# A four-layer graph network on one core: preparation split into four parts, waits dropped from the attention sweep, scan rows stored without gaps, and another release for the relation sweep's marks

## What is computed

```
L0: msg = relu([x[src], x[dst], w] @ W1 + b1) @ W2 + b2 ; agg = segment_max(msg, dst) ; relu([x, agg] @ U1 + c1) @ U2 + c2
L1: msg = relu([x[src], factors[dst]] @ Wm + bm)         ; agg = segment_sum(msg, src) ; x + relu([x, agg] @ Wc + bc)
L2: four heads: e = leaky_relu(e_l[src] + e_r[dst]) ; softmax of e over the edges of a receiver ; sum of alpha * Wh[src]
L3: twice: neigh = mean over edges of h[src] ; h = h @ W[0] + neigh @ W[1] (relu after the first)
```

## Time and profile before

| | us |
|---|---|
| median of 3 runs (lowest, highest) | 6593.26 (6587.62, 6595.1) |
| profiled execution: time | 6596.86 |
| profiled execution: span, first to last instruction | 6595.1 |
| busy: POOL, PE, DVE, ACT | 3886.5 (59%), 3682.2 (56%), 2495.9 (38%), 1392.2 (21%) |
| DMA, mean over the span | 165 GB/s |

### The profile page before, as it was taken

The page is one execution under the profiler, slowest core; times in us unless marked ns, Lnnn a source line. Parts: engine busy times, 40 slices in busy tenths (PEclk is TensorE's granted clock), DMA queues, the critical chain, the costliest instruction groups (busy, mean ns, idle before and its releaser), DMA issues. The chain is left out here.

```text
span 6595.1 us, 101052 instructions
## 1 busy us (share of the span) xinstructions
PE 3682.2 (56%) x19907; PEld 2827.0 (43%) x19907; DVE 2495.9 (38%) x4067; ACT 1392.2 (21%) x3059; POOL 3886.5 (59%) x3936
## 2 busy tenths in 40 slices
PE   1258888896587777636666564233333343333334
PEld 1145565564465555435555554123323332332332
DVE  4223333334344444525655555422222212222224
ACT  0012222222122232212222222111111111111111
POOL 0467777776200000667777774577777757777775
PEclk9679999998799999767878777555555565555556
DMA  9369999993355555256656563344544434444452
GB/s 343 123 193 293 291 296 292 298 297 105 122 182 182 186 182 171 81 124 171 168 156 168 156 169 103 92 126 125 127 126 125 126 86 126 125 127 126 125 127 75
DMA packets 1080339, 1090.67 MB, mean 165 GB/s; under 512 B 128353, under 2 KB 867622, under 8 KB 1076854
## 3 DMA queue, kind: packets, MB, share of 16 engines
q1 hardware_dynamic: 398532, 393.02, 20.3%
q10 hardware_dynamic: 546204, 390.09, 19.1%
q0 software_dynamic: 135456, 306.11, 18.5%
HBM read 662.62 MB, written 427.19 MB: 165 GB/s over the span
## 5 line engine op out<-in xcount | busy, mean ns | idle before, releaser
L1040 POOL DMA_INDIRECT gath<-sender_table,idx x1664 | 1657.6, 996 | 547.4 <-issue 376.0
L1247 DVE TENSOR_TENSOR_SCAN scan<-meta,scan,bank 128x512 f32<-128x512 bf16 x624 | 798.6, 1280 | 2086.1 <-DVEq L1244 2083.0
L1116 PE MATMUL bank<-ident,gath 128*128 128x128 f32 x1664 | 464.1, 434 | 1367.3 <-DMA gath<-sender_table,idx 1367.3
L1463 POOL DMA_INDIRECT gath<-attention_table,idx x832 | 852.3, 1024 | 349.3 <-issue 226.7
L1040 POOL DMA_INDIRECT gath<-joint_table,idx x832 | 850.3, 1022 | 273.6 <-issue 213.0
L1116 PEld LDWEIGHTS bank<-ident,gath 128*128 128x128 f32 x1664 | 297.7, 217 | 1533.4 <-DMA gath<-sender_table,idx 1533.4
L682 POOL COPY idx<-end_i 128x4 int32<-128x4 int32 (+1 forms) x65 | 13.5, 207 | 1040.5 <-POOLq L681 1040.3
L1184 ACT ACTIVATE rows<-bank 128x512 f32<-128x512 f32 x624 | 372.7, 597 | 1101.7 <-ACTq L1183 1059.1
L1142 PE MATMUL bank<-ident,scan 128*128 128x128 f32 x2496 | 570.1, 374 | 5.0 <-PEq L1140 5.0
L1142 PEld LDWEIGHTS bank<-ident,scan 128*128 128x128 f32 x2496 | 471.7, 203 | 132.0 <-issue 132.0
L1123 PE MATMUL bank<-ident,gath 128*128 128x128 f32 x1664 | 374.8, 310 | 0.0
(11 more groups left out here) (245 smaller groups left out, 6065.8 us busy)
## 6 DMA issues: line engine op xcount, KB each, us to landing
recv<-receiver_rows SPq DMA_DIRECT2D x624, 256.0 KB
scan_rows<-rows ACTq DMA_DIRECT2D x624, 256.0 KB
attention_scan_rows<-rows ACTq DMA_DIRECT2D x208, 264.0 KB
receiver_rows<-gath ACTq DMA_DIRECT2D x26, 2048.0 KB, 11.2
meta<-edge_meta SPq DMA_DIRECT2D x208, 256.0 KB
factor_rows<-gath ACTq DMA_DIRECT2D x208, 256.0 KB
gath<-factor_rows SPq DMA_DIRECT2D x208, 256.0 KB
scan_rows<-rows SPq DMA_DIRECT2D x208, 256.0 KB
```

Of the source, the lines that this page charges most:

```text
L1040: pool.indirect_dma_start(out=landed[s][:, c, 0:width], out_offset=None, in_=table[:, :], in_offset=bass.IndirectOffsetOnAxis(ap=idx[s][:, ...
L1116: ins = pe.transpose(b[:, c * P:(c + 1) * P], g[:, c, 0:F], ident[:, :])
L1247: chain(v.tensor_tensor_scan(scan[s % 2][:, :], go_on, src, scan[1 - s % 2][:, EB - 1:EB], ALU.add if k == 1 else ALU.mult, ALU.max if k = ...
L1463: pool.indirect_dma_start(out=gath[s][:, c, :], out_offset=None, in_=att_d[:, :], in_offset=bass.IndirectOffsetOnAxis(ap=idx[s][:, c:c + 1 ...
```

## The change

1. **Preparation in parts.** The 52 node tiles are taken in four parts (12, 14, 14, 12). DVE counts tiles of part g, releases POOL for part g's gathers, and then counts inside part g-1, on one semaphore per part. The edge marks and the rest stay.
2. **Scan rows put together.** Where only features are kept, `rows[s]` is written and stored as 4 x 128 floats without gaps (rows_flat), in edge phases 1, 4, 5 and the relation sweep.
3. **Relation sweep.** The marks are loaded right behind the wait on e_recv_free; e_meta_free is no longer used there. PE issues go_row before the senders.
4. **Attention sweep.** Marks and receiver rows share one wait on SP. The free semaphores of same, er, msg, hid, pre, scan and back are no longer raised or waited for, and scores no longer waits for its own end (one semaphore t_added is waited for once per stretch). PE and ACT take turn_back / keep_rows ahead of turn_weighted / keep_weighted; DVE takes scores ahead of same_receiver.

```
+        rows_flat = [r[:, :, :].rearrange("p c f -> p (c f)")[:, 0:CT * F].rearrange("p (c f) -> p c f", f=F) for r in rows]
...
+            quarter = (0, 12, 26, 40, NT)
...
+                    for g in range(4):
+                        pool.wait_ge(tiles_ready, 1)
+                        pool.sem_inc(tiles_ready, -1)
+                        for t in range(quarter[g], quarter[g + 1]):
+                            pool.indirect_dma_start(out=found[:, t, :], out_offset=None, in_=dst_d[:, :],
+                                                    in_offset=bass.IndirectOffsetOnAxis(ap=tiles_i[:, t:t + 1], axis=0),
+                                                    bounds_check=last_row, oob_is_err=False).then_inc(found_in[g], 16)
...
+                    def count_tiles(lo, hi):
...
+                        chain(v.tensor_scalar(tiles[:, lo:hi], tiles[:, lo:hi], float(T - 1), None, ALU.min))
+                        chain(v.tensor_copy(tiles_i[:, lo:hi], tiles[:, lo:hi]))
+                        v.sem_inc(tiles_ready, 1)
+
+                    def count_inside(lo, hi, g):
+                        v.wait_ge(found_in[g], 16 * (hi - lo))
...
+                    for g in range(5):
+                        if g < 4:
+                            count_tiles(quarter[g], quarter[g + 1])
+                        if g > 0:
+                            count_inside(quarter[g - 1], quarter[g], g - 1)
```

The relation sweep, SP's load and PE's steps:

```
-                        sp.wait_ge(e_meta_free, 1)
-                        sp.sem_inc(e_meta_free, -1)
-                        sp.dma_start(meta[s][0:1, 0:2, :], meta_d[0:2, part(q, s, SLOTS, EB)].unsqueeze(0)).then_inc(meta_in[s], 16)
-
                         sp.wait_ge(e_recv_free, 1)
                         sp.sem_inc(e_recv_free, -1)
+                        sp.dma_start(meta[s][0:1, 0:2, :], meta_d[0:2, part(q, s, SLOTS, EB)].unsqueeze(0)).then_inc(meta_in[s], 16)
...
-                    steps(pe, NB, SLOTS, (0, rank_row), (2, senders), (2, go_row), (4, turn_back))
+                    steps(pe, NB, SLOTS, (0, rank_row), (2, go_row), (2, senders), (4, turn_back))
```

The attention sweep, the steps of PE and ACT, and DVE's pieces (the free semaphores on PE's and ACT's side go in the same way):

```
-                    steps(pe, NB, U, (9, turn_weighted), (11, turn_back), (0, receiver_scores), (1, stretch))
+                    steps(pe, NB, U, (11, turn_back), (9, turn_weighted), (0, receiver_scores), (1, stretch))
-                    steps(act, NB, U, (9 + 7, keep_weighted), (11 + 7, keep_rows), (0, indices), (1 + 7, stretch))
+                    steps(act, NB, U, (11 + 7, keep_rows), (9 + 7, keep_weighted), (0, indices), (1 + 7, stretch))
-                        v.wait_ge(e_same_free, 1)
-                        v.sem_inc(e_same_free, -1)
...
-                        v.sem_inc(e_same_free, 1)
-                        v.sem_inc(e_meta_free, 1)
-                        chain(v.tensor_tensor(em[s // SB][:, lo:lo + CT * HEADS].rearrange("p (c h) -> p c h", h=HEADS),
-                                              gath[s][:, :, F:F + HEADS], er_ps[:, 0:CT * HEADS].rearrange("p (c h) -> p c h", h=HEADS), ALU.add))
-                        v.sem_inc(t_er_free, 1)
+                        v.tensor_tensor(em[s // SB][:, lo:lo + CT * HEADS].rearrange("p (c h) -> p c h", h=HEADS),
+                                        gath[s][:, :, F:F + HEADS], er_ps[:, 0:CT * HEADS].rearrange("p (c h) -> p c h", h=HEADS), ALU.add).then_inc(t_added, 1)
...
+                        v.wait_ge(t_added, SB)
+                        v.sem_inc(t_added, -SB)
...
-                        v.wait_ge(e_scan_free, 1)
-                        v.sem_inc(e_scan_free, -1)
...
-                        v.sem_inc(e_pre_free, 1)
-                        v.sem_inc(e_hid_free, 1)
...
-                    steps(v, NB, U, (9, weigh), (10, add_up), (0, same_receiver), (1, scores), (1, stretch))
+                    steps(v, NB, U, (9, weigh), (10, add_up), (1, scores), (0, same_receiver), (1, stretch))
```

More of the change, by code:

```diff
@@ new lines, in count_inside @@
+                    def count_inside(lo, hi, g):
+                        v.wait_ge(found_in[g], 16 * (hi - lo))
+                        v.sem_inc(v_done, 1)
+                        with v.Fori(lo // 2, hi // 2) as q:
+                            for u in range(2):
+                                v.wait_ge(v_done, 1)
+                                v.sem_inc(v_done, -1)
+                                v.tensor_scalar(junk[u][:, 0:P], found[:, bass.ds(q * 2 + u, 1), :], node_f[:, bass.ds(q * 2 + u, 1)], None, ALU.is_lt, ALU.add,
+                                                accum_out=inside[:, bass.ds(q * 2 + u, 1)]).then_inc(v_done, 1)
+                        v.wait_ge(v_done, 1)
+                        v.sem_inc(v_done, -1)
@@ L1088, in store @@
                         sp.sem_inc(e_rows, -1)
[L1089 removed]
+                        sp.dma_start(scan_d[part(q, s, SLOTS, EB), :].rearrange("(p c) f -> p c f", c=CT), rows_flat[s][:, :, :]).then_inc(stored[s], 16)
                     if expands:
```

67 lines of the change are left out of this document (16 added, 51 removed).

## The result

| | before | after |
|---|---|---|
| median, us (lowest, highest, runs) | 6591.85 (6587.62, 6595.1, 4) | 6308.39 (6299.61, 6324.83, 4) |
| profiled execution: time, span | 6596.86, 6595.1 | 6302.62, 6300.8 |
| busy: POOL, PE, DVE, ACT | 59, 56, 38, 21% | 62, 57, 40, 22% |

What follows compares the result with a forecast made beforehand. It took POOL's gathers to bound sweeps 4 and 5 and a loop of waits the relation sweep. Gains 56 + 169 + 85 + 12 = 322 us off 6596.9 gave 6275, set to 6271 for the runs' median; range 6215 to 6400.

Steps and rivals of the forecast that it cites:

- the overlap that was worked out: Preparation: DVE's counts run beside POOL's gathers in four parts, so start_f comes at 212 us; gain 56 us.
- The loop of 4.2 us through SP's load of the marks: Relation sweep: scan, marks' load and rank row wait in a circle that sets the pace; cutting it gains 169 us.
- What is late next?: Relation sweep with the loop cut: DVE's own step of 3.38 us per block, with PE near at 3.39.
- The allowance to 3.45: Relation sweep: pace set a little above DVE's 3.38 and PE's 3.39 us, as engines so near rarely interlock without loss.
- (a): Rival: part of the loops closes again; relation sweep gains 87 us, attention 40; time 6404 us; chance 0.21.
- (b): Rival, relation sweep: the marks were never the bound, SP's early load does nothing; time 6440 us; chance 0.05.
- (d): Rival, PE in relation sweep: go row closes a one-step loop, 6.9 us per block; 6985 us; chance 0.03, other standstills included.
- so DVE's lap falls to 42.0 and meets POOL's 41.6: Attention sweep, eight blocks: lap falls from 45.6 us, taken as 42.2; gain 85 us, bounds 40 and 119.
- The price of the semaphores: Attention sweep: dropped raises and waits, some 0.11 us each, shorten DVE's step by 0.45 us per block, 3.6 per lap.
- The gap at the jump back: Attention sweep: DVE stands 5.2 us once in two laps, likely instruction fetch; losing it could add some 10 us.
- The floor taken from sweep 4: POOL's pace of 1.301 us per gather in phases 4 and 5, taken as floor for every phase that gathers.
- I take 12: First sweep: longer stored pieces cost ACT's queue less; gain 12 us, bounds 0 and 25.

Runs made afterwards that it cites:

- run 7: Changed kernel with nine more semaphore instructions of DVE per block in the attention sweep, which do nothing; 6425.84 us.
- run 6: Changed kernel with the whole attention sweep as before the change; 6392.57 us.
- run 2: Changed kernel with the scan rows kept apart and stored in 512-byte pieces again; 6312.42 us.
- run 4: Changed kernel with the relation sweep as before: marks released by the scan and PE's senders ahead of the go row; 6467.88 us.
- run 12: Changed kernel with three more useless DVE semaphore instructions per block in the attention sweep; 7416.64 us on a slower chip, ratio 0.9599 to the kernel before.
- runs 1 and 10: Changed kernel with preparation in one part again, 6355.97 us; and with same-receiver by four tensor_scalar in first and attention sweeps, 7582.0 us on a slower chip.
- run 9: Changed kernel with three unread DVE sums per block in sweeps 4 and 5; 7511.2 us on a slower chip, ratio 0.9648 to the kernel before.
- run 10: Changed kernel with same-receiver by four tensor_scalar in first and attention sweeps; 7582.0 us on a slower chip, ratio 0.9760 to the kernel before.

## Why the prediction was right, and where not

**Preparation: right.** 213.4 us against 212, by the overlap that was worked out; undoing it moves start_f by 55.9 us.

**Relation sweep: right in mechanism, 13 us too much.** The loop of 4.2 us through SP's load of the marks was the bound: with its release back the pace is 4.31. The answer DVE to "What is late next?" held, and its 3.38 us were met exactly in three blocks of four. The allowance to 3.45 was for PE and DVE interlocking. What there is instead is 0.57 us at each jump back of DVE's loop over four blocks: 3.38 + 0.57 / 4 = 3.52, the pace found. PE costs nothing. Rivals (a) and (b) fall, and (d), for PE's waits for the go row are 35.6 us in all.

**Attention sweep: nearly the right sum, by errors that cancel.** The step that failed is "so DVE's lap falls to 42.0 and meets POOL's 41.6". The price of the semaphores held, though its terms add up to 0.37 us (three times 0.11, and 0.24, less 0.2) and not to the 0.45 stated: DVE's bare step fell by 0.46 us, and in run 7 an instruction costs 0.10. The gap at the jump back, set aside with the page's rule for 10 us at most, went as well: 51.7 us in the trace of before, 47.8 in run 6. Together that is nearly 150 us of DVE's time (an estimate: 208 x 0.46 + 52), and 77 came out. The rest turned into waits of DVE, ahead of its scan (58.9 us, 22.9 before) and for gathers (32.9 us). How much of the 77 either cause would give alone, no run shows. What stops the gain is POOL: between 2750 and 3700 us it never stands for a slot and needs 43.4 us for 32 gathers, not 41.6 (DVE's laps, 42.6 us, are shorter only since DVE starts a ring of slots behind POOL and catches up). The floor taken from sweep 4 is no constant. Of the 66 us that the 1147 us of this sweep's gathers have over the 1081 of sweep 4, 46 are gathers held up by DVE's operations on two SBUF operands (874.9 against 1657.1 / 2 = 828.5) and 20 are idle time, nearly all of it one wait of 20.2 us when the ring of slots first fills. The collisions were already there before (59 slow gathers), and are more now that DVE and POOL run closer (149). That 85 lies near 77 is luck.

**Scan rows put together: wrong.** "I take 12" rested on "at most the 42 us above the floor can go". The queue's price per byte did fall, to 20.9 GB/s per engine, but run 2 puts the part at 4 us or nothing. What sets the first sweep's pace is not shown. By POOL's busy time 25 of its 40 us over the floor are held-up gathers (854.0 against 828.5), yet the pace does not follow them (run 4 has 848.7 us of busy time and a pace of 1.363); its DMA engines are 93% busy. The Trainium skill's line rate from 512 bytes (DMA: Bandwidth & Descriptors, Specifications) gave the right time; the trace's queue rows still differ by piece size.

**The whole.** The mechanisms of the two largest terms were right, and the forecast was 37 us too low: 13 in the relation sweep, 10 in the first, 8 in attention, 1 in the preparation, the rest between the medians and the traces.

## What to carry to other kernels

A few instructions more in a loop's body can cost more than all that they do: look at the idle time put down to "issue" at a loop's jump back before pricing the instructions in the loop, and try the body a few instructions shorter, or a short loop written out longer. When a loop of waits is cut, work out the next engine's bare step from the same rows; it is the pace to expect, plus its jump back, and look which other engine then has no waits left. POOL's floor taken from a phase without DVE operations on two SBUF operands does not hold in a phase with them.

## What the runs showed of the hardware

- A loop of DVE with 307 recorded instructions jumps back without idle time, one with 339 stands for 4 to 6 us each time (run 12); ScalarE's with 327 does not.
- A jump back of DVE's short loop (63 recorded instructions) added 0.57 us to the step in the changed kernel, and 0.33 us in runs 1 and 10 with the same loop.
- A recorded semaphore instruction of DVE took 0.10 us of its step where nothing covered it (run 7).
- A gather takes POOL 0.996 us. Where it starts while DVE computes a tensor_tensor from two SBUF operands, it takes longer by what is left of that operation less 0.13 us, up to 0.5 us. One PSUM operand avoids it wholly (0 of 277 that started under such a sum, run 9). So did a tensor_scalar from bf16 with a column as its scalar in the first sweep (0 of 832, run 10), but not every tensor_scalar: of 20 gathers of the node phases that start under the one from float32 (L838), 3 are slow in the changed kernel.
- The same kernel, the one before, took 18% longer on one chip than on another (7794 and 6590 us). The edited kernels there show equal instruction times and 22 to 24% less traffic per second in the first sweep.
